# The causal mask of the row scores, moved into two stack columns and four quarter-array matmuls

## What is computed

```
scores = jnp.einsum('bhqd,bhkd->bhqk', q, k_h) / math.sqrt(HEAD_DIM)
causal = jnp.triu(jnp.ones((t, t), dtype=bool), k=1)
scores = jnp.where(causal[None, None], jnp.finfo(scores.dtype).min, scores)
attn = jax.nn.softmax(scores, axis=-1)
ctx = jnp.einsum('bhqk,bhkd->bhqd', attn, v_h)
```

## Time and profile before

| | |
|---|---|
| median of 3 runs | 1218.53 us |
| the profiled execution | 1219.86 us, its span 1218.1 us |
| mean granted TensorE clock | 0.986 |
| TensorE matmul busy | 1144.7 us (94%) |
| VectorE, ScalarE, GpSimd busy | 772.1, 655.0, 502.0 us |
| mask matmuls L872 | 768, 57.8 us busy |
| row-score matmuls L863 | 1024, 102.6 us busy |

### The profile page before, as it was taken

One profiled execution on the slowest core, in us unless ns is written; L12 is line 12 of the kernel. 1 busy time (PEld: TensorE's weight loads), 2 busy tenths in 40 slices (PEclk: granted clock), 3 DMA queues, 4 the chain that ended last, 5 costly groups with the idle time before them and its releaser, 6 DMA issues.

```text
span 1218.1 us, 22076 instructions
## 1 busy us (share of the span) xinstructions
PE 1144.7 (94%) x8476; PEld 843.3 (69%) x8476; DVE 772.1 (63%) x1124; ACT 655.0 (54%) x1199; POOL 502.0 (41%) x648
## 2 busy tenths in 40 slices
PE   5999999999999999989999999999899999998997
PEld 4788876776656565556687888777677767676665
DVE  7843457785865746684644465545788777775545
ACT  4434347675555655564332333325867676776654
POOL 0000026564422212124555544432775566646552
PEclk8999989999999999999999999999999999999999
DMA  7000010030000100001243222210100101010001
GB/s 277 1 1 1 1 36 2 2 116 2 2 1 2 40 1 1 27 28 53 78 132 102 91 91 78 78 61 5 51 3 2 44 2 34 5 40 12 2 2 69
DMA packets 15258, 48.04 MB, mean 39 GB/s; under 512 B 2858, under 2 KB 6959, under 8 KB 14388
## 3 DMA queue, kind: packets, MB, share of 16 engines
q1 hardware_dynamic: 15156, 46.63, 11.4%
HBM read 44.00 MB, written 2.10 MB: 38 GB/s over the span
## 4 chain that ended last, share of the span: by engine, by line
PE 74%; DVE 12%; ACT 7%; issue 4%; DMA 2%; POOL 1%; DVEq 0%; ACTq 0%; SPq 0%; POOLq 0%
PE bank L679 18%; PE bank L812 16%; PE bank L712 9%; PE bank L950 8%; PE bank L925 6%; PE bank L863 4%; DVE negmax L1906 4%; PE bank L905 4%; ACT probs L1446 3%; DMA W_lo_whole<-in_w 2%; PE bank L872 2%; PE bank L829 1%; PE bank L630 1%; DVE W_lo_whole L1676 1%; ACT qT L1418 1%
## 5 line engine op out<-in xcount | busy, mean ns | idle before, releaser
L1906 DVE TENSOR_REDUCE negmax<-bank 128x4 f32<-128x1024 f32 (+1 forms) x256 | 250.5, 1017 | 100.1 <-PE bank L872 80.2
L1446 ACT ACTIVATE probs<-bank 128x512 f32<-128x512 f32 (+1 forms) x224 | 188.2, 847 | 52.4 <-PE bank L905 51.0
L2139 POOL TENSOR_SCALAR_AFFINE_SELECT probs<-probs 128x512 f32<-128x512 f32 x192 | 123.3, 648 | 169.1 <-ACT probs L1446 167.7
L2061 POOL TENSOR_TENSOR W_lo<-W_lo_whole,W_hi 128x512 fp32r<-128x512 f32 x84 | 117.3, 1425 | 100.0 <-ACT W_hi L1175 100.0
L925 PE MATMUL bank<-probs,V 128*32 128x256 f32 (+1 forms) x2048 | 117.3, 347 | 8.2 <-ACT probs L1446 4.5
L1175 ACT ACTIVATE W_hi<-W_lo_whole 128x1536 fp32r<-128x1536 f32 x28 | 41.7, 1489 | 130.7 <-DVE W_lo_whole L1676 130.7
L863 PE MATMUL bank<-kT,qT 64*128 64x256 f32 (+1 forms) x1024 | 102.6, 296 | 9.7 <-DVE xT_lo L1557 3.5
L905 PE MATMUL bank<-qT,kT 64*128 64x256 f32 (+1 forms) x512 | 97.2, 395 | 11.0 <-ACT qT L1418 4.1
L1457 ACT ACTIVATE pv<-bank 128x256 f32<-128x256 f32 x128 | 49.8, 389 | 97.7 <-PE bank L925 97.7
L925 PEld LDWEIGHTS bank<-probs,V 128*32 128x32 f32 x2048 | 53.6, 109 | 63.9 <-issue 28.5
L863 PEld LDWEIGHTS bank<-kT,qT 64*128 64x128 f32 x1024 | 79.0, 188 | 22.8 <-issue 7.7
(11 more groups left out here) (214 smaller groups left out, 2668.1 us busy)
## 6 DMA issues: line engine op xcount, KB each, us to landing
W_lo_whole<-in_w SPq DMA_DIRECT2D x28, 768.0 KB, 4.2
Wqkv_lo_whole<-in_Wqkv SPq DMA_DIRECT2D x6, 768.0 KB, 6.9
Wo_lo_whole<-in_Wo SPq DMA_DIRECT2D x4, 1024.0 KB, 5.3
Wqkv<-in_Wqkv SPq DMA_DIRECT2D x2, 1536.0 KB, 7.9
Wdown_whole<-in_Wd SPq DMA_DIRECT2D x1, 2816.0 KB, 14.6
x<-in_x SPq DMA_DIRECT2D x4, 512.0 KB, 6.4
out<-x SPq DMA_DIRECT2D x8, 256.0 KB, 2.0
V_lo_whole<-in_V SPq DMA_DIRECT2D x1, 1408.0 KB, 6.2
```

What stands on the lines that cost most here:

```text
L1446: nc.scalar.activation(A[l].probs[gi % 2][kb][:, :, q0 - kb * A[l].probs1:].rearrange("p (b h) q -> p b h q", b=2), B.tensor(key)[:, :, 0: ...
L1906: v.tensor_reduce(A[l].negmax[u % 2][:, qb, :].rearrange("p (b h) -> p b h", b=2)[:, :, 2 * g:2 * g + 2], B.tensor(key)[:, :, 0:2 * nk].re ...
L2061: ins = gp.tensor_tensor(lo, whole, hi.bitcast(F32), ALU.subtract)
L2139: gp.affine_select(out=blk, in_=blk, compare_op=ALU.is_ge, fill=0.0, base=0, pattern=[[0, 4], [1, P]], channel_multiplier=-1).then_inc(cau ...
```

## The change

The mask of the row scores is split in two. In a diagonal block of 128 queries by 128 keys, the quarter with queries 0 to 63 and keys 64 to 127 is masked whole; this quarter now comes out of the score matmul itself: one more column of the query stack holds 1 for the first 64 queries of a tile, and the matching column of the key stack -2^100 for the last 64 keys (column 49 for the first tile, 50 for the second). The two triangles on the diagonal are added by matmuls of 64 stationary by 2x64 moving columns, each in its own quarter of the array (64*64): the upper or lower 64 partitions in, the first or last 64 query partitions out.

```diff
-NEG = -1.0e30
+NEG = -2.0 ** 100
...
                     for j in range(2):
                         for par in range(2):
                             half = slice(64 * par, 64 * par + 64)
+                            dst = ps[64 * j:64 * j + 64, par, 0:2 * nk].rearrange("p (h k) -> p h k", h=2)
                             k0 = nk - P + 64 * j
-                            dst = ps[:, par, 0:2 * nk].rearrange("p (h k) -> p h k", h=2)[:, :, k0:k0 + 64]
-                            ins = mm(dst, cut_rows[half, j, :], cut_keys[half, j, :, :], start=False, stop=(j == 1))
+                            ins = mm(dst[:, :, k0:k0 + 64], cuts[half, 0, :], cuts[half, 1:3, :], start=False, stop=True)
...
-                        v.tensor_copy(cut_rows[:], cut_rows_f[:]).then_inc(mask_set.sem, 1)
-                        v.tensor_copy(cut_keys[:], cut_keys_f[:]).then_inc(mask_set.sem, 1)
+                        v.tensor_copy(cuts[:], cuts_f[:]).then_inc(mask_set.sem, 1)
...
-                    gp.memset(A[l].kstack[i][:, :, :, STACK:STACK + 1].bitcast(F32), 1.0).then_inc(pads.sem, 1)
-                    gp.memset(A[l].kstack[i][:, :, :, STACK + 1:64].bitcast(F32), 0.0).then_inc(pads.sem, 1)
+                    kr = A[l].kstack[i][:].rearrange("p n h s -> p (n h) s")
+                    ks = kr.bitcast(F32)
+                    gp.memset(ks[:, :, STACK:STACK + 1], 1.0).then_inc(pads.sem, 1)
+                    c = STACK + 1
+                    if CAUSAL[l]:
+                        if i == 1:
+                            gp.memset(ks[:, :, c:c + 1], 0.0).then_inc(pads.sem, 1)
+                        c += i
+                        gp.tensor_copy(kr[:, :, c], half_marks[:, 1:2].to_broadcast([P, 2 * A[l].kn])).then_inc(pads.sem, 1)
+                        c += 1
+                    gp.memset(ks[:, :, c:64], 0.0).then_inc(pads.sem, 1)
...
-                    gp.memset(A[l].qstack[i][:, :, STACK:64].bitcast(F32), 0.0).then_inc(pads.sem, 1)
+                    qs = A[l].qstack[i][:].bitcast(F32)
+                    c = STACK + 1 + i
+                    gp.memset(qs[:, :, STACK:c], 0.0).then_inc(pads.sem, 1)
+                    gp.tensor_copy(A[l].qstack[i][:, :, c], half_marks[:, 0:1].to_broadcast([P, UH])).then_inc(pads.sem, 1)
+                    gp.memset(qs[:, :, c + 1:64], 0.0).then_inc(pads.sem, 1)
...
             pool.wait_ge(*B.filled(("up", 0, 1, 4)))
+            pool.wait_ge(const_in, 16 * CONSTS)
             set_pads(0)
...
-            for dst, name in [(cut_rows_f, "cut_rows"), (cut_keys_f, "cut_keys")] + [(cosT[l], f"cos{l}") for l in (0, 2, 3)] + \
+            for dst, name in [(cuts_f, "cuts"), (half_marks, "half_marks")] + [(cosT[l], f"cos{l}") for l in (0, 2, 3)] + \
```

More of the change, by code:

```diff
@@ L271, in program @@
         ident_r = place("ident_r", [P, P], F32R)
-        cut_rows = place("cut_rows", [P, 2, P], BF16)
-        cut_keys = place("cut_keys", [P, 2, 2, 64], BF16)
+        cuts = place("cuts", [P, 5, 64], BF16)
+        half_marks = place("half_marks", [P, 2], F32)
         cosT = {l: place(f"cos{l}", [P, 2, HD], F32) for l in (0, 2, 3)}
@@ L407, in program @@
         ones = place("ones", [P, P], F32, at)
-        cut_rows_f = place("cut_rows_f", [P, 2, P], F32, at)
-        cut_keys_f = place("cut_keys_f", [P, 2, 2, 64], F32, at)
+        cuts_f = place("cuts_f", [P, 5, 64], F32, at)
         sign_in = place("sign_in", [P, KC, OCT], F32, at)
@@ L517, in program @@
         ones_set = mark("ones_set", [3, 0, 0, 0])
-        mask_set = mark("mask_set", [3, 0, 0, 0])
+        mask_set = mark("mask_set", [2, 0, 0, 0])
         ln_stat = mark("row_stats", [TILES] * 4)
@@ L565, in program @@
         stack_lo = mark("stack_lo", [32] * 4)
-        PADS = [6 + 4 * 4, 4, 6 + 3 * 4, 0]
+        PADS = [6 + 7 + 4 * 4, 4, 6 + 7 + 3 * 4, 0]
         pads = mark("pads_set", PADS)
@@ L794, in project @@
                 if u == 0 and tau == 0:
-                    pe.wait_ge(*mask_set.at(0, 3))
+                    pe.wait_ge(*mask_set.at(0, 2))
                 pe.wait_ge(*B.emptied(("xT", l, t)))
@@ L2358, in layouts @@
     r = np.arange(64)
[L2359 to L2367, removed]
+    cuts = np.zeros((64, 5, 64), np.float32)
+    cuts[r, 0, r] = 1
+    cuts[:, 1:3] = np.where(r[None, :] > r[:, None], np.float32(NEG), np.float32(0))[:, None, :]
+    cuts[:, 3:5] = np.where(r[None, :] < r[:, None], np.float32(NEG), np.float32(0))[:, None, :]
+    second = np.arange(P) >= 64
+    o["half_marks"] = np.stack([np.where(second, 0.0, 1.0), np.where(second, NEG, 0.0)], 1).astype(np.float32)
+    o["cuts"] = np.concatenate([cuts, cuts])
     which, sign = octonion_table()
```

## The result

The changed kernel takes 1245.33 us (median of 4 runs, 1243.76 to 1246.95), the kernel before 1215.84 us beside it (4 runs). The ratio is 1.0231, with a 95% interval of 1.0203 to 1.0259: slower by 28 us by the ratio (the medians of these few runs lie 29.5 us apart). 33 us were forecast.

A forecast was written before the change was run, and what follows sets the result against it. TensorE, busy 94% of the span, was taken to bound the kernel. Entering, loads, streaming and leaving summed to 36.6 us on TensorE, times 0.9 = +33 on 1218.5: 1251 us, range 1215 to 1268.

The forecast's parts named there:

- Entering the shape: From 64*128 scores to 64*64 masks: array empties, +0.09 us per block, and the masks' own weights load uncovered, +0.02.
- the first rival: No stop between 64*128 and 64*64, which share their rows; only the masks' streaming counts: 1210 us, chance 0.16.
- The quarters' streaming: Four quarters of the array take all four masks at once: 0.10 us becomes 0.05, -0.05 per block.
- Rival 3: Stops come but quarters gain nothing, the second mask pair still waiting for the first: 1262 to 1270 us, chance 0.10.
- Leaving, with the shorter masks: From the masks to the next shape: today's 0.10 us, less 0.05 streaming, plus 0.12 for the change of shape.
- The exposed load behind it: After leaving the masks' shape, the next matmuls' weights load in the open: +0.02 us per block, bounds 0.02 and 0.11.
- The sum on TensorE: +0.20 us for 179 blocks followed by a 64*128 matmul, +0.06 for the 13 others: together 36.6 us.
- Rival 2: The stop is half covered by weight loads already in the open around the masks: 1235 us, chance 0.14.
- Stacks, pads, constants: Stack columns, GpSimd's seven more pads before layers 0 and 2, and the constants' copy and transfers cost nothing.
- What passes on to the end: In the mask stretches TensorE idles 6%, so 0.9 of time added to its sequence shows in the end.
- The 53 ns that the prediction put in on trial: Load of 64 bf16 columns for the quarter masks, tried in place of 0.02 us: estimate 5 us higher.

The follow-up runs named there:

- one-column kernel: Kernel before plus one 64*64 quarter matmul of one zero moving column ahead of the masks in each of 192 blocks: 1246.18 us, ratio 1.0221.
- the first experiment: The changed kernel with its triangle matmuls in the scores' tile shape (128 stationary columns, 64 of them zero), stacks and pads kept: 1217.3 us, ratio 1.0.

## Why the prediction was right, step by step

- **Entering the shape**, forecast 0.09 + 0.02: measured 0.10 in the slot, 0.09 in the feed-forward net, 0.08 for one column alone. The row used, 128*128 to 128*32, was the right neighbour: a shape that shares its rows with the one before still stops the array. This was the open point and the reason for the first rival (1210 us), which fell.
- **The quarters' streaming**, forecast -0.05: measured 0.06 for four more masks against 0.11, so -0.05. Rival 3 (nothing gained, 1262 to 1270) fell.
- **Leaving, with the shorter masks**, forecast 0.10 - 0.05 + 0.12 = 0.17: measured 0.18. The exposed load behind it, +0.02, is inside the 0.10 of the `qb` 1 groups: they take 0.43 in the change, where a stop stands ahead of them, and 0.41 in the one-column kernel, where the old masks stand between that stop and them.
- **The sum on TensorE**, forecast 36.6 us: by the steps 179 x 0.19 and 13 x 0.05, 35 us; its busy time grew by 33.0 us over before and by 34.8 over the first experiment, whose clock is like the change's (0.990 and 0.989).
- **Rival 2** (the stop half hidden by loads that are in the open anyway, 1235): nothing of it was hidden there.
- **Stacks, pads, constants**, forecast nothing: nothing (0.9975 to 1.0025).
- **What passes on to the end**, forecast 0.9: this term was a little high. 28 us of 35 is 0.8; the interval of the ratio allows 0.7 to 0.9, so the runs alone put 0.9 at the edge. The prediction said that idle time falling by much more than a tenth of what is added would show it; in the two stretches that answer to the earlier trace rows

```profile
153.00:275.00 122.00, 116.68 (x1139) 84.71 (x1138) 86.96 (x131) 78.37 (x164) 60.52 (x90) 0.97 0.10 34
780.00:1160.00 380.00, 362.78 (x3312) 261.37 (x3310) 254.18 (x387) 235.77 (x473) 209.50 (x281) 0.99 0.07 25
```

  TensorE is idle for 5.3 and 17.2 us, where it was for 6.2 and 23.6: 7 us, a fifth of what was added. A share of idle time (6%) need not be the share of a delay that it absorbs: a delay in every slot can shorten each wait of TensorE for a follower that stands behind it. This is the likely reason; no run isolates it. Taking work away passed on even less, 6 us of 20.

The profiled pair differs by 23.9 us only, less than the medians. A part of that goes with the clock of the profiled execution of before. Its stretch, that of the change, and that of the change in the old tile shape (us, PE busy, granted clock, DMA share and GB/s):

```profile
170.00:175.00 5.00, 4.08 (x32) 0.52 0.00 0
175.00:180.00 5.00, 5.00 (x25) 0.50 0.02 5
```

```profile
170.00:175.00 5.00, 3.48 (x42) 0.96 0.01 2
175.00:180.00 5.00, 4.72 (x25) 0.50 0.00 0
```

```profile
170.00:175.00 5.00, 3.32 (x44) 1.00 0.00 0
175.00:180.00 5.00, 5.00 (x57) 1.00 0.02 3
```

Before ran these 10 us at or near 0.50, which is 1.2 GHz, the change 5 of them, the third none. TensorE had been busy 3.63, 4.26 and 3.93 us of the 5 us ahead of 170, so that does not tell them apart. Against the span of the third, 1215.3 us, the change is 26.7 us longer, 0.77 of the 34.8 us that its TensorE is busy longer.

## What to carry to other kernels

Count changes of tile shape on TensorE before you split a small matmul into quarters: here each way into another shape and out of it cost 0.2 us together, while the quarters saved 0.05. If a narrower tile shape is to pay, several such matmuls have to stand together at a place where the shape changes anyway; eight here just broke even within a slot, and no run had more. And check a follower's waits before you count on what a shorter TensorE sequence gives back.

## What the hardware showed that was not expected

- One matmul of one moving column, 192 times, cost 27 us (1.0221) in another tile shape and nothing (0.9992) in the same one.
- In this kernel the way out takes the same time whichever of two shapes follows: 0.18 us from the quarter masks to a 64*128 load in f32 (921.98 to 922.16) and to a 128*128 one (808.30 to 808.48).
- A load of 64 bf16 columns in a quarter is not shorter than one of 128 columns. Instructions of the masks in the change, to be held against the earlier trace rows:

```profile
L871 PEld LDWEIGHTS bank<-cuts x768: 102/103/125, 154.5 to 1150.2; 64*64 64x64 bf16 x192
L871 PE MATMUL bank<-cuts x768: 240/240/313, 154.5 to 1150.2; 64*64 64x128 bf16 x192
```

  103 ns at the median, 96 before. The 53 ns that the prediction put in on trial is not what this trace shows. The short loads cost little all the same: entering took 0.08 to 0.10 us, no longer than the forecast of 0.11, which had 0.02 for them.
